# A stack of four graph layers: staged sums in the last two passes, spread padding of the edge list, and counting with 16-bit compares

## The reference

```python
h = relu(layernorm(x));  x = x + L0(h)   # three rounds of attention over edges, 4 heads
h = relu(layernorm(x));  x = x + L1(h)   # edge softmax, a scan over nodes sorted by degree, gate, feed-forward
h = relu(layernorm(x));  x = x + L2(h)   # see below
h = relu(layernorm(x));  x = x + L3(h)

# L2
neighbor = segment_sum(edge_val[:, None] * h[src], dst)
out = (h @ W1.T + b1) + (neighbor + neighbor * h) @ W2.T + b2
out = where(out >= 0, out, 0.2 * out);  out / max(norm(out), 1e-12)
# L3
relu(h @ W + segment_sum((h @ M)[src], dst))
```

## Time and profile before

| | us |
|---|---|
| median of 3 runs | 8496.55 (8486.33 to 8499.98) |
| the profiled execution | 8437.77 |
| its span | 8436.0 |
| PE, DVE, ACT, POOL busy | 5542.8, 5075.4, 3299.4, 4451.5 |
| gathers of L2 | 5459.5 to 6893.3 |
| gathers of L3 | 6961.5 to 8374.2 |
| last collect of L3 | 8405.0 |

### The profile page before, as it was taken

One profiled execution on the slowest core, in us unless ns is written; L12 is line 12 of the kernel. 1 busy time (PEld: TensorE's weight loads), 2 busy tenths in 40 slices (PEclk: granted clock), 3 DMA queues, 4 the chain that ended last, 5 costly groups with the idle time before them and its releaser, 6 DMA issues. The chain is left out here.

```text
span 8436.0 us, 108263 instructions
## 1 busy us (share of the span) xinstructions
PE 5542.8 (66%) x20087; PEld 3496.7 (41%) x20087; DVE 5075.4 (60%) x10802; ACT 3299.4 (39%) x11053; POOL 4451.5 (53%) x4404
## 2 busy tenths in 40 slices
PE   4757688888886466577777657645556654555555
PEld 4524344444443232344444445424434432334443
DVE  7769488888887535588888746434444442323332
ACT  1224566666664247688888744300000000000000
POOL 4230365566553530667777632266656646666664
PEclk9978899999998567799999889867777776677777
DMA  7132688888886633788888942233333353333335
GB/s 246 26 84 94 217 274 272 276 274 278 274 277 200 206 116 111 260 299 301 312 301 291 268 128 72 67 94 110 115 111 114 116 89 94 106 111 113 111 112 82
DMA packets 532219, 1477.04 MB, mean 175 GB/s; under 512 B 134848, under 2 KB 226252, under 8 KB 531211
## 3 DMA queue, kind: packets, MB, share of 16 engines
q0 software_dynamic: 239680, 842.82, 34.1%
q1 hardware_dynamic: 249532, 561.11, 18.9%
q10 hardware_dynamic: 42668, 69.51, 2.6%
HBM read 1196.53 MB, written 607.81 MB: 214 GB/s over the span
## 5 line engine op out<-in xcount | busy, mean ns | idle before, releaser
L1222 POOL DMA_INDIRECT rows_e<-bundle,unit_src x1856 | 1762.7, 950 | 1161.6 <-issue 491.5
L1243 PE MATMUL acc_e<-rows_e,hot_e 128*128 128x256 f32 x3712 | 1265.6, 491 | 1056.4 <-issue 534.4
L618 POOL DMA_INDIRECT rows_e<-table,unit_src x928 | 1027.6, 1107 | 879.6 <-PE acc_e L823 448.5
L1243 PEld LDWEIGHTS acc_e<-rows_e,hot_e 128*128 128x128 f32 x3712 | 837.0, 244 | 1453.0 <-issue 1104.6
L1000 POOL DMA_INDIRECT rows_e<-table,unit_src x928 | 1040.1, 1121 | 481.6 <-issue 251.7
L812 ACT ACTIVATE rows_e<-rows_e 128x64 f32<-128x64 f32 x4640 | 1118.9, 332 | 1.9
L1252 DVE SCALAR_TENSOR_TENSOR sums_e<-sums_e,unit_keep,acc_e 128x256 f32<-128x256 f32 x928 | 443.8, 478 | 1056.1 <-remote 556.6
L2422 ACT ACTIVATE turned_f<-turn_f 128x512 f32<-128x512 f32 x98 | 58.5, 597 | 2278.6 <-DMA given_f<-bundle 1132.7
L1084 ACT ACTIVATE rows_e<-rows_e 128x64 f32<-128x64 f32 x3712 | 925.0, 333 | 25.5 <-issue 20.5
L823 PE MATMUL acc_e<-rows_e,unit_w 128*128 128x512 f32 (+1 forms) x1856 | 714.3, 532 | 146.8 <-issue 112.8
L823 PE MATMUL acc_e<-rows_e,hot_e 128*128 128x512 f32 (+1 forms) x1856 | 639.0, 497 | 33.9 <-ACT rows_e L812 26.9
(11 more groups left out here) (457 smaller groups left out, 9249.7 us busy)
## 6 DMA issues: line engine op xcount, KB each, us to landing
bc<-bc_rows SPq DMA_DIRECT2D x228, 896.0 KB
summed<-sums_e SPq DMA_DIRECT2D x464, 390.0 KB
bundle<-sums_e SPq DMA_DIRECT2D x928, 128.0 KB
summed<-sums_e SPq DMA_DIRECT2D x464, 130.5 KB
given_f<-bundle ACTq DMA_DIRECT2D x98, 384.0 KB
rows_e<-table,unit_src POOLq DMA_INDIRECT x1856
hots<-hot_e SPq DMA_DIRECT2D x116, 256.0 KB
hots<-unit_w SPq DMA_DIRECT2D x116, 256.0 KB
```

Of the source, the lines that this page charges most:

```text
L618: pool.indirect_dma_start(self.rows[:, v, e, :], None, table, bass.IndirectOffsetOnAxis(unit_src[:, u, e:e + 1], 0)).then_inc(self.landed[ ...
L1222: pool.indirect_dma_start(self.rows[:, v, e, :], None, self.tab, bass.IndirectOffsetOnAxis(unit_src[:, u, e:e + 1], 0)).then_inc(self.land ...
L1243: mm = pe.matmul(self.acc[:, v % 2, 0:D], self.hot[:, v % self.SUMS, e, :], self.rows[:, v, e, :], start=(e == 0), stop=(e == 1))
```

## The change

It has four parts.

- L2 and L3: the sums are 16 deep. There is no condition on a store: after each eight units one DMA of 1 MB writes eight sums to a DRAM tensor `stage`, in the order of the units. A second table, `ends`, gives the last unit of each block, and the posts load the sum from `stage` and the other two parts from `bundle`, which is two parts wide instead of three. `interact` starts its later steps after the seventh unit of a half-round instead of the fifth.
- The padding of the sources names 128 zero rows in turn.
- The counting compares 16-bit numbers; the eight indices are the innermost axis of the one-hot matrices, so that PE reads them with a step of 16 bytes.
- The sum part of `bundle` is no longer cleared (98 DMAs of POOL).

```diff
-                for hot, of, width in ((self.hot_low, self.low, P), (self.hot_high, self.high, T)):
-                    dve.tensor_tensor(hot[:, b, :, :], iota[:, 0:width].unsqueeze(1).broadcast_to([P, QB, width]),
-                                      of[:, ds(n * QB, QB)].unsqueeze(2).broadcast_to([P, QB, width]),
+                for hot, of, wide, width in ((self.hot_low, self.low, self.wide_low, P), (self.hot_high, self.high, self.wide_high, T)):
+                    dve.tensor_tensor(hot[:, b, :, :], wide[:, :, :], of[:, n * QB:(n + 1) * QB].unsqueeze(1).broadcast_to([P, width, QB]),
                                       ALU.is_equal).then_inc(self.made, 1)
...
-                    mm = pe.matmul(self.counts, self.hot_low[:, b, k, :], self.hot_high[:, b, k, :],
+                    mm = pe.matmul(self.counts, self.hot_low[:, b, :, k], self.hot_high[:, b, :, k],
...
-            SUMS = 8
+            SUMS, HOTS = RING, 8
...
                 u, at_ = i * RING + v, v % self.SUMS
                 dve.wait_ge(self.s_pe, u + RING + 1)
-                dve.wait_ge(self.stored[at_], 16 * (2 * i + v // self.SUMS + 1))
+                if v % UB == 0:
+                    dve.wait_ge(self.staged[v // UB], 16 * (i + 1))
...
-                u = i * RING + v
-                block = sp.value_load(unit_block[0:1, ds(u, 1)], min_val=0, max_val=SKIP)
+                if v % UB < UB - 1:
+                    return
+                u, half = i * RING + v, v // UB
                 sp.wait_ge(self.s_sum, u + 3)
-                sp.dma_start(self.bundle[:, 0:D][ds(block * P, P), :], self.sums[:, v % self.SUMS, :],
-                             cond=(block < SKIP)).then_inc(self.stored[v % self.SUMS], 16)
+                sp.dma_start(stage[:, ds(u - UB + 1, UB), :], self.sums[:, half * UB:(half + 1) * UB, :]).then_inc(self.staged[half], 16)
...
                 if steps:
-                    for b in range(self.SUMS):
-                        act.wait_ge(self.stored[b], 16 * (2 * i + half))
+                    for h in range(2):
+                        act.wait_ge(self.staged[h], 16 * (i + max(half, 1 - h)))
                         act.sem_inc(act_passed, 1)
...
-                    steps = [(early(one, j), 4, 3)]
+                    steps = [(early(one, j), 6, 3)]
...
+            def load_block(ch, j, bundle):
+                block, end = block_of(j), block_of(j, ends, UNITS)
+                return ch.move(lambda e: e.dma_start(given[:, 1:3, :].rearrange("p k d -> p (k d)"), bundle[ds(block * P, P), :]),
+                               lambda e: e.dma_start(s3, stage[:, ds(end, 1), :].rearrange("p o d -> p (o d)")))
```

More of the change, by code:

```diff
@@ L214, in graph_stack_kernel @@
         h_dram = scratch("h_dram", [ROWS, D])
-        bundles = [scratch(f"bundle{k}", [(SKIP + 1) * P, 3 * D]) for k in range(2)]
+        bundles = [scratch(f"bundle{k}", [ROWS, 2 * D]) for k in range(2)]
+        stage = scratch("stage", [P, UNITS + 1, D])
         x_dram = scratch("x_dram", [NP, D])
@@ L1205, in __init__ @@
                 self.landed, self.seen = landed, seen
-                self.stored = [sem(f"stored_{name}{v}") for v in range(self.SUMS)]
+                self.staged = [sem(f"staged_{name}{h}") for h in range(2)]
                 self.s_hot, self.s_pe, self.s_sum = (sem(f"{n}_{name}") for n in ("hot", "pe", "sum"))
@@ L1209, in __init__ @@
                 dve.sem_inc(self.s_sum, 2)
-                for v in range(self.SUMS):
-                    sp.sem_inc(self.stored[v], 16)
+                for h in range(2):
+                    sp.sem_inc(self.staged[h], 16)
                 chain.step(dve, lambda: dve.memset(self.sums[:, self.SUMS - 1, :], 0.0))
@@ L1325, in run @@
                     self.store_sums(n - 1, v)
-                for v in range(self.SUMS):
-                    act.wait_ge(self.stored[v], 16 * (UNITS // self.SUMS + 1))
+                for h in range(2):
+                    act.wait_ge(self.staged[h], 16 * (self.ROUNDS + 1))
                 for j in range(2 * n - self.AFTER, T + 1):
@@ L1402, in count_beside @@
                     targets.products(n, n % 2)
-                    for _ in range(2):
-                        next(clearing, None)
+                    next(clearing, None)
                     yield
@@ L1530, in plan_units @@
                                                              ALU.mult, ALU.add))
+            yield chain.apart((dve, lambda: dve.tensor_scalar(none[:, :], cols[:, 0:1], 0.0, None, ALU.is_equal)),
+                              (dve, lambda: dve.tensor_scalar(ends_f[:, :], begins[:, 1:2], -1.0, float(UNITS + 1), ALU.mult, ALU.add)))
+            yield chain.step(dve, lambda: dve.tensor_tensor(none[:, :], none[:, :], ends_f[:, :], ALU.mult))
+            yield chain.step(dve, lambda: dve.scalar_tensor_tensor(ends_f[:, :], begins[:, 1:2], -1.0, none[:, :], ALU.add, ALU.add))
             yield chain.step(dve, lambda: dve.tensor_copy(cols[:, 0:1], lane[:, :]))
@@ L1539, in plan_units @@
             yield chain.step(pe, lambda: pe.matmul(small[0:1, 256:256 + T], lane[0:T, 0:1], pair[0:T, 0, :], start=True, stop=True))
+            yield chain.step(pe, lambda: pe.matmul(small[0:1, 320:320 + T], ends_f[0:T, 0:1], pair[0:T, 0, :], start=True, stop=True))
             yield chain.step(pe, lambda: pe.matmul(row_ps[:, :], named[0:T, :], past[0:T, :], start=True, stop=True))
@@ L2309, in graph_stack_kernel @@
             top = lsb("top", [P, 1])
[L2310 removed]
+            chain.step(dve, lambda: dve.tensor_scalar(unit_src[:, :, :], unit_src[:, :, :], 1, None, ALU.logical_shift_left))
             chain.step(dve, lambda: dve.tensor_scalar(top[:, :], top_neg[:, :], -1.0, None, ALU.mult))
```

68 lines of the change are left out of this document (37 added, 31 removed).

## The result

The changed kernel takes 8544.5 us (5 runs, 8530.1 to 8558.7), before 8496.6; the ratio is 1.0058 with a 95% interval of 1.004 to 1.0077. The forecast was 8100 us, with 0.05 for slower. The profiled execution took 8530.1 us, with a span of 8528.2, 92 us more than that of before.

A forecast was written before the change was run, and what follows sets the result against it. SP's instructions for each unit were taken to pace L2 and L3, alternating with DVE's chain in L2. Terms -40 -20 -32 -28 -126 -27 -128 +5 = -396 took the profiled 8437.8 to 8042; with 58.8 carried over, 8100 us; 80% range 7990 to 8310.

The forecast's parts named there:

- term 4: L2 and L3: removing SP's instructions for each unit shortens rounds; -28 and -126 us in L2, -27 and -128 in L3.
- rival 2: L2 and L3: slow sequencers stay, rounds of 47 to 48 us, about -220 us in all, 8280; chance 0.25.
- a part I called harmless: L2: interact's last five DVE steps in a row after the eighth unit, its first two units later; no separate price.
- Posts' half left over: L2 and L3 rounds with posts: half the loss above POOL's floor stays, giving 45.0 and 42.7 us a round.
- rival 1: L2 and L3: all rounds reach POOL's floor of 40 to 41 us, about -570 us, 7930; chance 0.17.
- Rival 3: L2 and L3: the 1 MB store lands late and sets the half-round, 8670 us; chance 0.05.
- Rival 4: Counting: compares stay slow or PE's strided reads double; terms 1 and 2 give -10, 8150; chance 0.10 with the forecast's rest.
- Term 1: Counting beside stage 0: 16-bit compare pairs take 1.04 us instead of 1.78, clears priced at nothing; -40 us (0 to -77).
- Term 2: Counting beside the plan, 300 to 930 us: cheaper compares save -20 us (+3 to -50).
- Term 3: Padding gathers at the passes' ends get cheaper with different rows: -15 us in L3, -12 in L1, -5 in L2.
- theory H: Formed after the first trace: PE's signals arrive late while POOL gathers without a break, so the posts' chain's place sets the loss.

The follow-up runs named there:

- groups 3 to 5: Follow-up runs on chips where the kernel before takes 7827, 7833 and 7826 us.
- before_k6: Kernel before with the early posts' later steps from the seventh slot of a half-round instead of the fifth: ratio 1.015 to before.
- staged_k4: Changed kernel with the early posts' later steps from the fifth slot in both passes instead of the seventh: 8471 us, ratio 1.0011 to before.
- count_pad: Kernel before with only the 16-bit counting and the spread padding; clears, L2 and L3 as before: ratio 0.9775 to before.
- store_small: Changed kernel storing one sum of eight (128 KB instead of 1 MB), posts reading a fixed slot: ratio 1.0056 to before.
- before_pause: Kernel before with a clear of a 128x256 tile on POOL ahead of each unit's gathers in L2 and L3: ratio 1.0227 to before.
- after_again: The changed kernel itself, run again in group 4, where before takes 7833 us: ratio 0.9796 to before.
- count_pad_2: Kernel before with only the 16-bit counting and spread padding, repeated in group 4, where before takes 7833 us: ratio 0.9782 to before.
- first pair: The first measurement of both kernels: before 8496.6 us, changed 8544.5 us.
- groups 1 and 2: The first follow-up runs, on chips where the kernel before takes 8462 and 8494 us.
- slots_4_6: Changed kernel with the early posts' later steps from the fifth slot in L2 and the seventh in L3: ratio 0.9925 to before.
- pool_pause: Changed kernel with a clear of a 128x256 tile on POOL ahead of each unit's two gathers in L2 and L3: 8356 us, ratio 0.984, one run.

## Why the prediction was wrong

- **The step that failed** is the reading that SP is the pace-maker in L2 and L3 (term 4): `remote` before the collect was taken for SP's release of `stored`, because SP waited for DVE only 16.0 us. On that chip SP and DVE were both slow for a third reason. With SP relieved, rounds without posts went from 46.9 to 46.5 us where I had 42.5, and in L3 `remote` stayed at 245.1 us. What the runs put in its place: on that chip PE's signals arrive late while POOL issues gathers, at ACT by a median of up to 12.5 us, at POOL by some 10 us in the half-round shown. Shown are the lags, that they end with POOL's last gather, that they go with its issues and not with their bytes, and that they are absent on the chips of groups 3 to 5, where SP does its work for each unit and still waits for DVE half of the time. That `remote` before the collect is the same lateness fits all of this, and is argued. I had the sign in hand: rival 2 spoke of slow phases with POOL's unbroken issuing, but priced them at the sequencers alone and not at what other engines wait for.
- **The size and the sign** of term 4 in L2 come from a part I called harmless: "interact's last five DVE steps now stand in a row", its first "later by two units". That number alone costs 5.7 us a round on the kernel before (before_k6), about 126 us in 22 rounds, against 4.9 us a round in the changed kernel, and with the number back 3.9 of these are gone (staged_k4). I had judged it by ACT's spare time and not by what DVE has behind `o_f` on its queue.
- **Posts' half left over** (45.0 and 42.7 us a round): no run took these values. Where nothing is late posts cost nothing, 40.1 to 40.4 us; rival 1, POOL's floor, is what the second kind of chip does, and before must do it there too, since its code of L2 and L3 is count_pad's (40.1), though no trace of it was taken there. So even there the staged part gains nothing.
- **Rival 3** (the 1 MB store) is out: store_small, and the collect of the changed kernel has no wait for `stage`. **Rival 4** was half right. The compare now costs (686 - 355) / (1024 - 392) = 0.52 ns an element, half of the 1.04 of before. The Trainium skill's rule ("VectorE: DVE Perf Modes", What auto-detection actually checks) agrees with 686 and 355 ns. PE's strided reads cost 23% a weight load and 26% a product, where I had nothing from rows 10. The Trainium skill's rule on lines of 16 bytes ("SBUF — State Buffer", Specifications), which I had set below rows 10, agrees in sign.
- **Term 1** came to -30 us instead of -40, with PE now the busiest engine. More than half of it is the clears, which I priced at nothing: count_pad keeps them, and its last one-hot of the stage starts at 236.8 us, where before_pause has 250.6 and after_again, without clears, 219.8. The counting itself is worth 14 us there. By L0's first gather the clears' share is gone again (865.6 in count_pad, 866.9 in after_again). **Term 2**: the first gather of L0 is 40 us earlier in all, for 60 predicted; on the second kind of chip 60 (926.0 in before_pause, 865.6 in count_pad).
- **Term 3** holds on the first chip. The last rounds of L1 and L3 went from 69.6 and 63.4 us to 51.2 and 48.6, -18 and -15 for -12 and -15; L2's did not move (49.4 to 50.1). On the second kind of chip it was too small: by before_pause and count_pad L1's last round is 19 us shorter (64.0 and 45.3), and the stretches behind the last gathers of L1, L2 and L3 are 20, 23 and 38 us shorter. That is 100 us for the 32 of the term, if all of it is the padding.
- **The sum** by the two traces: -40 to the first gather of L0, +41 from there to the last of L1, -10 to L2, +108 in L2, -7 from there to the end: +92. Two sums of the rivals were off as written: the parts of rival 1 add up to 583 and not 570, those of rival 2 to 207 and not 220; neither changes a reading. On the second kind of chip the staged part is worth nothing either way (after_again 0.9796, count_pad_2 0.9782) and the other parts are the whole -2%.
- **The range** (7990 to 8310) held neither result: the same change is +0.6% on one chip and -2.0% on another, and 0.9796 of 8496.6 would be 8323 us.

What stays open: why PE's signals are late, whether a break in POOL's issuing lets them through, and why they are late where the first pair and groups 1 and 2 ran and not where groups 3 to 5 did. The late ones all ran first, so a difference of hour can't be told from one of chip. Also why L2 likes the fifth slot and, with staged sums, L3 the seventh: theory H says that the place matters, but not which. And L2 and L3 take 46 to 47 us a round on these chips even without posts, where no place of the posts' chain can matter.

## What to carry to other kernels

An engine that is always late is not yet the one that sets the pace: ask what would be seen if it and its waiters were slowed by the same thing, and take one waiter whose releaser is certain (here ACT's copy behind PE's transposes) to measure the lag itself. Where a chain of other engines' work stands in an engine's order, its place against the long run of a neighbour can be worth more than the work removed: two slots were worth 1.5% of the kernel before, on one chip. And run a change of a few per cent on more than one chip before it is believed, since its sign can turn.

## What the runs showed of the hardware that was not expected

- On one kind of chip the same kernel takes 8462 to 8496 us, on another 7826 to 7833, with POOL's gathers at 953 ns and DVE's collects at 480 ns on both. The difference is in waits: in L2 and L3 lags from PE's end to ACT's start with medians of up to 12.5 us, and single register operations of 0.7 or 1.4 us beside a median of 53 ns.
- The lag goes with POOL's issuing of gathers: it is the same (11.0 us) with a quarter of the bytes, small (1.8 and 0.04) with half the issues, and 0.04 in all 80 copies behind POOL's last gather of a pass. The clear of 0.33 us between pairs of gathers brought its median to 0.04 in L2, but not in L3 (3.6), and left the collect's `remote` in L2's rounds without posts as it was.
- PE's weight loads and products with operands 16 bytes apart take 146 and 276 ns against 119 and 219 for contiguous 16-bit ones, while float32 weights 48 bytes apart cost nothing.
- No single version is best on both: slots_4_6 and pool_pause beat before where signals are late (0.9925, and 0.984 in one run), and there the changed kernel is slower than before (1.0058); where they are not late, the clear only costs (before_pause 1.0227), and count_pad_2 (0.9782) and the changed kernel (0.9796) have overlapping intervals.
